# Token stage of a two-layer gated block: x2 turned as it is, routing logits from two sources, and new queue orders on all engines

## The chip, the cores and the metric

One core of a Trainium2 chip runs the kernel. The metric is device time in microseconds (us), the median of several runs. Names: TensorE (PE in the rows; PEld are its weight loads), VectorE (DVE), ScalarE (ACT), GpSimd (POOL), SyncE (SP, DMA queues). Semaphores order the engines; each engine works through its own queue in order.

## The reference, cut to what matters

All is fp32: x is (4, 2048, 512), ctx (4, 77, 512).

```python
x = x + tanh(g_xattn[0]) * memory_update(ctx, layernorm(x))   # a shift of rows, a strided convolution, ctx appended
x = x + tanh(g_ffn[0]) * quantised_linear(layernorm(x))       # blocks of 32 to a 6-bit grid, x @ w.T + bias   -> x2
Up = relu(layernorm(x) @ U_w.T); Uq = D_param * relu(ctx @ U_w.T)
x = x + tanh(g_xattn[1]) * softmax(mask(Up @ Uq.T)) @ ctx     # -> x3
t = layernorm(x)
idx, pmax = argmax, max of softmax(t @ Wr)                    # 8 experts
# each expert takes its first 1280 tokens; others keep t
x = x + tanh(g_ffn[1]) * pmax * (relu(t @ W1[idx]) @ W2[idx]) # or + tanh(..) * t for those without a place
```

## The kernel before

The kernel has a set-up, a token stage and an expert stage. The expert stage (`exp`, lines 1292 to 1790) is not touched. It starts when all engines have ended the block of the token stage.

**Token stage.** 8192 tokens go in 16 groups of 512, each as four tiles of 128 rows (T = 4). A software pipeline of six stages holds six groups at once: in step t, z is group t, a is t-1, b is t-2, c is t-3, d is t-4, e is t-5 (`groups`, line 198). Every engine has one `body(z, a, b, c, d, e)`, and `pipeline` (line 205) runs it: some steps written out, steps 6 to 15 as a loop, then the last five written out. Stage z normalises `xs`; a adds it to X, normalises into `n1` and quantises; b does the quantised linear and gives x2; c makes `up`; d scores, softmax and attention and gives x3; e writes t and x3 to memory and routes.

Products are split into fp32r high and low parts: ScalarE copies the high part out of PSUM, VectorE subtracts to get the low part, and TensorE multiplies three times (`split_terms`, line 713).

**TensorE's queue** in a step (`body`, line 721, order from about line 812): scores of d turned into p_sc (L727); `linear` x4 for b (12 products each, L710); `al` turned (L816); `attend` x4 for d; `turn_input` x4 for e (L718: four transposes each of the normalised `tt`); `project` x4 for c (12 products each, L780), with the fp32 `logits` of e (L763) inside `project(1)`; `turn_normed` x4 for b (the normalised `n2`, L718); positions of e (L838 to L842); scores of c (L710); `turn_quantised` x4 for a (L718).

**ScalarE's queue** (`body`, line 565): exponential of d, `alT_hi`, `tt` normalised, `n1` normalised, copies of the turned tiles (L574, L592), `up` (L583), `xs` normalised ahead of `up(1)` (L638), `n2` normalised, y, then the copies of the last turned tiles and `sT` (L669).

**VectorE's queue** (`body`, line 963): softmax sums, moments of d, a, c and b (`moments`, line 918: four `bn_stats` and four `bn_aggr`), the additions that make x2 (L974) and x3 (L987), quantisation (L1095 to L1108), low parts (L997, L1006), routing of e (L1074 to L1126), slots of the group before (`slots_of`, line 937).

**POOL** (line 473): X + xs (L480), slots scattered (L469), X + bias (L488), then dequantising `n1` (L494). **SP** loads `xs` and X when X + xs and x3 are done (`load_group`, line 361).

After the last step TensorE sums the counts (L914), and VectorE builds the tables of the expert stage (L1232 to L1281).

**Set-up** (lines 216 to 298 and the parts ahead of each `pipeline`): U_w and the linear weight are turned and split, keys `uq` and their low parts made, the convolution done.

## Time and profile before

| | us |
|---|---|
| median of 3 runs | 2196.72 (2196.54 to 2197.13) |
| the profiled execution | 2196.92 |
| its span, first to last instruction | 2194.6 |
| granted TensorE clock over the span | 0.961 of full speed |
| start to the first attention step | 172.3 |
| token stage up to the start of the experts | 874.7 |

The times in the rows are those of one profiled execution. "Idle before" is the time that an engine stood ahead of an instruction, with what released it. The duration of a matmul includes its way through the array, so what a matmul costs in a queue is the distance between starts. A clock of 1.00 is 2.4 GHz, 0.50 is 1.2 GHz.

### The profile page before, as it was taken

How to read it: one execution, taken by the hardware profiler on the slowest of the kernel's cores; microseconds unless marked ns; L12 is line 12 of the kernel's file. 1: busy time of each engine (PE TensorE's matmuls, PEld its weight loads, DVE VectorE, ACT ScalarE, POOL GpSimd, SP SyncE). 2: the span in 40 equal slices, each digit the busy share in tenths (PEclk: the TensorE clock that was granted, in tenths of full speed). 3: DMA queues.
4: the chain of work that ended last, by engine and by line, in shares of the span. 5: the costliest groups of instructions: out<-in, count | busy, mean ns of one | idle time of the engine just before them, and what ended most of it. 6: DMA issues, size and time to landing. Idle time of an engine off the chain costs nothing.

```text
span 2194.6 us, 35464 instructions
## 1 busy us (share of the span) xinstructions
PE 1982.1 (90%) x11356; PEld 1692.3 (77%) x11357; DVE 1043.4 (48%) x2321; ACT 794.8 (36%) x1548; POOL 670.9 (31%) x579
## 2 busy tenths in 40 slices
PE   4468998899889975799999999999999999999997
PEld 2456776677667754698988998899889899899986
DVE  3478888998899744424241115122413313322241
ACT  1254656555665443324141114111413313311241
POOL 0534243434353302415051115111513313301250
PEclk9689999999999985899999999999999999999999
DMA  6311333333333423615051004201512403301130
GB/s 190 112 61 43 122 130 121 116 120 140 115 120 121 146 85 117 197 32 185 20 183 43 29 29 156 69 29 38 183 43 91 129 29 96 120 19 38 54 112 16
DMA packets 152243, 208.41 MB, mean 95 GB/s; under 512 B 12831, under 2 KB 78623, under 8 KB 152198
## 3 DMA queue, kind: packets, MB, share of 16 engines
q1 hardware_dynamic: 111125, 114.14, 16.3%
q0 software_dynamic: 15728, 43.38, 6.5%
q10 hardware_dynamic: 25344, 50.33, 6.3%
q8 instruction: 22, 0.36, 0.1%
q14 instruction: 24, 0.19, 0.0%
HBM read 140.98 MB, written 68.37 MB: 95 GB/s over the span
## 4 chain that ended last, share of the span: by engine, by line
PE 58%; ACT 0%; issue 0%; DMA 0%; POOL 0%; POOLq 0%; DVEq 0%; ACTq 0%; DVE 0%
PE bank L1646 23%; PE bank L1654 22%; PE bank L1619 5%; PE bank L1599 5%; PE bank L1577 1%; PE bank L1608 1%; DMA tg<-t_d,idx_t 0%; ACT w_hi L1510 0%; PE bank L1583 0%; ACT w_hi L1511 0%; POOLq L1351 0%; DMA slots<-slot_d 0%; POOL out_dram L1389 0%; DVEq L1292 0%; ACT inT_hi L1496 0%
## 5 line engine op out<-in xcount | busy, mean ns | idle before, releaser
L1737 DVE SCALAR_TENSOR_TENSOR hT_lo<-bank,hT_hi 128x256 fp32r<-128x256 f32 x352 | 149.0, 423 | 657.0 <-ACT hT_hi L1541 657.0
L1541 ACT ACTIVATE hT_hi<-bank 128x256 fp32r<-128x256 f32 x352 | 135.1, 384 | 747.8 <-PE bank L1646 747.8
L1646 PE MATMUL bank<-inT_hi,w_lo 128*128 128x256 f32 x1408 | 398.5, 283 | 0.0
L1646 PE MATMUL bank<-inT_lo,w_hi 128*128 128x256 f32 x1408 | 398.3, 283 | 0.0
L1646 PE MATMUL bank<-inT_hi,w_hi 128*128 128x256 f32 x1408 | 396.8, 282 | 0.0
L1654 PE MATMUL bank<-w_hi,hT_hi 128*128 128x512 f32 x704 | 279.9, 398 | 0.0
L1646 PEld LDWEIGHTS bank<-inT_hi,w_hi 128*128 128x128 f32 x1408 | 269.0, 191 | 13.3
L1646 PEld LDWEIGHTS bank<-inT_lo,w_hi 128*128 128x128 f32 x1408 | 269.0, 191 | 12.0
L1654 PE MATMUL bank<-w_lo,hT_hi 128*128 128x512 f32 x704 | 277.7, 394 | 0.0
L1654 PE MATMUL bank<-w_hi,hT_lo 128*128 128x512 f32 x704 | 274.1, 389 | 0.0
L1646 PEld LDWEIGHTS bank<-inT_hi,w_lo 128*128 128x128 f32 x1408 | 269.0, 191 | 0.0
L1389 POOL DMA_INDIRECT out_dram<-ob,idx_x x46 | 46.5, 1010 | 633.9 <-DVE ob L1747 617.5
L1399 POOL TENSOR_TENSOR w_lo<-stage,w_hi 128x512 fp32r<-128x512 f32 x112 | 159.9, 1444 | 79.8 <-ACT w_hi L1510 79.7
L1654 PEld LDWEIGHTS bank<-w_hi,hT_lo 128*128 128x128 f32 x704 | 132.3, 188 | 30.1
L1654 PEld LDWEIGHTS bank<-w_hi,hT_hi 128*128 128x128 f32 x704 | 133.5, 190 | 17.4
L1654 PEld LDWEIGHTS bank<-w_lo,hT_hi 128*128 128x128 f32 x704 | 133.6, 190 | 15.2
L718 PE MATMUL bank<-ident,n 128*128 128x128 f32 x512 | 79.8, 290 | 72.0 <-POOL n L494 40.3
L469 POOL DMA_INDIRECT slot_d<-pay,flat x64 | 62.6, 979 | 266.2 <-DVE flat L959 251.6
L494 POOL TENSOR_TENSOR n<-q,s 128x512 f32<-128x512 fp8e4 x64 | 83.5, 1332 | 188.0 <-DVE q L1108 188.0
L1711 DVE TENSOR_TENSOR w_lo<-stage,w_hi 128x512 fp32r<-128x512 f32 x128 | 133.3, 1054 | 0.0
L718 PEld LDWEIGHTS bank<-ident,n 128*128 128x128 f32 x512 | 59.9, 148 | 93.8 <-issue 66.1
L780 PE MATMUL bank<-n2T_hi,uw_hi 128*128 128x512 f32 x256 | 110.2, 430 | 13.3 <-DVE up_lo L997 13.3
(266 smaller groups left out, 3931.5 us busy)
## 6 DMA issues: line engine op xcount, KB each, us to landing
stage<-in_L_ffn_W_dram SPq DMA_DIRECT2D x256, 256.0 KB, 3.6
...
```

What stands on the lines that cost most here:

```text
L469: pool.indirect_dma_start(out=slot_d, out_offset=bass.IndirectOffsetOnAxis(ap=flat[:, j:j + 1], axis=0), in_=pay[:, j, :], in_offset=None, ...
L494: pool.tensor_tensor(n1[:, j, :].rearrange("p (n c) -> p n c", c=BLK), q8[:, j, :].rearrange("p (n c) -> p n c", c=BLK), s64[:, j, :].unsq ...
L718: last = pe.transpose(dst_bank[:, k * P:k * P + P], src[:, j, k * P:k * P + P], ident[:, :])
L780: last = pe.matmul(u_banks[h % 2][:, :], l, rows_t, start=(k == 0 and n == 0), stop=(k == KB - 1 and n == 2))
L1399: pool.tensor_tensor(w1_lo[:, :, fs], w1_block(f), w1_hi[:, :, fs].bitcast(F32), ALU.subtract).then_inc(e_split[f % RING], 1)
L1541: act.activation(hT_hi[:, f % 4, :], hb[f % 4][:, 0:CN], ACT.Relu).then_inc(e_hh, 1)
L1599: last = pe.matmul(first_bank[q % 2][:, :], l[:, k, :], r[:, k, qs], start=(n == 0), stop=(n == 3 * KB - 1))
L1619: last = pe.matmul(unit_acc[:, :], l[:, q % 2, f, :], r[:, q * FQ + f, :], start=(q == 0 and n == 0), stop=(q == NF - 1 and n == 3 * FQ - 1))
L1646: last = pe.matmul(hb[f % 4][:, 0:CN], l[:, k, fs], r[:, k, :], start=(n == 0), stop=(n == 3 * KB - 1))
L1654: last = pe.matmul(acc[i][:, :], l[:, f % 4, js], r[:, f, :], start=(f == 0 and n == 0), stop=(f == FB - 1 and n == 2))
L1711: dve.tensor_tensor(w2_lo[:, f, :], w2_block(f), w2_hi[:, f, :].bitcast(F32), ALU.subtract).then_inc(e_split[f % RING], 1)
L1737: dve.scalar_tensor_tensor(out=hT_lo[:, f % 4, :], in0=hb[f % 4][:, 0:CN], scalar=0.0, in1=hT_hi[:, f % 4, :].bitcast(F32), op0=ALU.max, o ...
```

## The change

- **Normalised copies.** `n2` and the turned `tt` go. TensorE turns x2 itself (`turn_second`, from X). The mean is taken out of U_w and Wr in the set-up (their rows are centred), so products of x2 equal those of x2 less its mean. The factor 1/std of c is put into the scale of the softmax's exponential.
- **Statistics.** `bn_stats` of c and d go. The additions that make x2 and x3 also write their row sums (`accum_out`), and ScalarE sums squares of x minus mean (`squares`) and makes 1/std from them.
- **Logits.** They are the sum of two parts: turned x2 times centred Wr (`q_la`, 32 fp32r matmuls of 16 columns inside `project(1)`, for c) and the attention's weights times a table `cwr` = ctx @ Wr made in the set-up (`q_lb`, two matmuls in each `attend`). Argmax, one-hot, positions and counts are done with d, a step earlier than before; only 1/sum, slots and scatter stay with e.
- **Softmax.** Four exponentials read PSUM directly with a bias and a scale and give their sums.
- **Banks.** Attention has two PSUM banks, x2's turned tiles four.
- **Orders.** On all engines, below. VectorE now runs: scaled logits and y's factors of e, `add_linear(0)`, maximum of d, sum and slots of e, `add_linear(1)`, moments of a's X, `alT_lo` and softmax factors, `add_linear(2)`, `add_attention(0)`, `add_linear(3)`, `add_attention(1)`, quantisation with `up_rest(0)` in it, `add_attention(2)`, `up_rest(1)`, `add_attention(3)`, moments of `xs`, `up_rest(2)`, `a_m` and its like, routing of d, low parts of the quantised tiles with `up_rest(3)` after the second, those of x2, positions. POOL dequantises before it adds the bias, and scatters the slots of e in e's own step.
- **TensorE's steps** are all written out; it has no loop. The steps of the others are as before.
- **Set-up.** Two passes of ScalarE over `uf` ahead of its transposes; sums of keys and of Wr over partitions on TensorE; `uqf` from three VectorE operations instead of one; the table `cwr` (32 small matmuls) with its split.

```diff
+l_banks = q_banks = bank[1], bank[2]
+u_banks = bank[3], bank[0]
+o_banks = bank[5], bank[6]
+x_banks = bank[5], bank[6], bank[3], bank[0]
+b_s, b_sm = bank[4], bank[7]
+q_la = b_sm[:, 320:320 + T * 2 * E].rearrange("p (j w) -> p j w", j=T)
+q_lb = b_sm[:, 384:384 + T * 2 * E].rearrange("p (j w) -> p j w", j=T)
+p_pos = b_sm[:, 448:448 + T * E].rearrange("p (j e) -> p j e", j=T)
...
+def squares(x, g, nm, sq, s, told, spare):
+    wait(act, told, g + 1)
+    wait(act, s, T * g)
+    settled(act)
+    for j in range(T):
+        act.activation(spare[:, j, :], x(j).rearrange("p o d -> p (o d)"), ACT.Square, bias=nm[:, j:j + 1],
+                       accum_out=sq[:, j:j + 1]).then_inc(s, 1)
+def rstd_of_squares(kind, g, sq, s, rs):
+    wait(act, s, T * (g + 1))
+    act.activation(lv[kind][:, :], sq[:, :], ACT.Ln, bias=eps[:, :], scale=1.0 / D).then_inc(a_rs[kind], 1)
+    wait(act, a_rs[kind], 2 * g + 1)
+    settled(act)
+    act.activation(rs, lv[kind][:, :], ACT.Exp, scale=-0.5).then_inc(a_rs[kind], 1)
...
+    wait(act, v_re, 3 * e + 1)
+    act.activation(re_[:, :, :], rsc[:, :, :], ACT.Exp).then_inc(a_re, 1)
+    wait(act, v_ys, 3 * e + 1)
+    wait(act, s_t, 16 * e)
+    settled(act)
+    for j in range(T):
+        act.activation(tt[:, j, :], x3[:, ds(xe + j, 1), :], ACT.Identity, bias=nb_d[:, j:j + 1],
+                       scale=rs_d[:, j:j + 1]).then_inc(a_tt, 1)
 if d is not None:
+    wait(act, v_sm, 3 * d + 2)
+    settled(act)
+    for j in range(T):
+        act.activation(al[:, j, :], p_sc[:, j, :], ACT.Exp, bias=nbx[:, j:j + 1],
+                       scale=rs_c[:, ds((d % T) * T + j, 1)], accum_out=ssm[:, j:j + 1]).then_inc(a_al, 1)
+if e is not None:
+    wait(act, a_tt, T * (e + 1))
+    act.dma_start(t_d[ds(er, G), :].rearrange("(j p) e -> p j e", p=P), tt[:, :, :]).then_inc(s_t, 16)
 if d is not None:
     wait(act, p_ca, d + 1)
     wait(act, p_co, T * d)
+    wait(act, p_lb, d)
     act.activation(alT_hi[:, :], b_s[0:L, :], ACT.Copy).then_inc(a_th, 1)
 if a is not None:
     rstd("b", a)
     wait(act, v_ln["b"], LN * (a + 1))
     wait(act, p_bt, T * a)
     normed("b", n1, lambda j: X[:, ds((a % T) * T + j, 1), :], a_n1)
 if e is not None:
     if d is not None:
         wait(act, v_x3, T * d + 1)
     act.dma_start(x3_d[ds(er, G), :].rearrange("(j p) e -> p j e", p=P),
                   x3[:, ds(xe, T), :]).then_inc(s_x3, 16)
+    wait(act, v_ys, 3 * (e + 1))
     wait(act, s_y, 16 * e)
     settled(act)
     for j in range(T):
         act.activation(y[:, j, :], x3[:, ds(xe + j, 1), :], ACT.Identity, bias=y_nb[:, j:j + 1],
                        scale=y_sc[:, j:j + 1]).then_inc(a_y, 1)
+up(0)
+if e is not None:
     wait(act, a_y, T * (e + 1))
     act.dma_start(of[ds(er, G), :].rearrange("(j p) e -> p j e", p=P), y[:, :, :]).then_inc(s_y, 16)
+if b is not None:
+    squares(lambda j: X[:, ds((b % T) * T + j, 1), :], b, nm_c, sq_c, a_sq, v_nm, junk)
+up(1)
+if b is not None:
+    rstd_of_squares("c", b, sq_c, a_sq, rs_c[:, ds((b % T) * T, T)])
+up(2)
+if d is not None:
+    squares(lambda j: x3[:, ds((d % 2) * T + j, 1), :], d, nm_d, sq_d, a_sd, v_nd, junk_d)
+if z is not None:
+    rstd("a", z)
+up(3)
+if d is not None:
+    rstd_of_squares("d", d, sq_d, a_sd, rs_d[:, :])
+if z is not None:
+    wait(act, v_ln["a"], (LN + 2) * (z + 1))
+    for j in range(T):
+        act.activation(xs[:, j, :], xs[:, j, :], ACT.Identity, bias=ln["a"][3][:, j:j + 1],
+                       scale=a_sc[:, j:j + 1]).then_inc(a_u, 1)
+for j in range(T):
+    quantised_hi(j)
+for j in range(T):
+    second_hi(j)
 if c is not None:
     wait(act, p_cs, c + 1)
     wait(act, p_cr, c)
     act.activation(sT[:, :], b_s[0:L, :], ACT.Identity, bias=maskb[:, ds(c, 1)]).then_inc(a_st, 1)
...
+    wait(pe, v_bl, T * b + (j + 3 if j < 2 else j + 1))
...
+        if d > 0:
+            wait(pe, v_r, 8 * (d - 1) + 1)
+    if j >= 2:
+        wait(pe, v_x3, T * d + j - 1)
+    elif c is not None:
+        wait(pe, v_cl, T * c + j + 1)
+    product(o_banks[j % 2][:, :], split_terms(alT_hi[:, js], alT_lo[:, js], cxb[:, 0, :], cxb[:, 1, :])
+    pe.matmul(q_lb[:, j, :], alT_hi[:, js], cwr[:, d // NQ, :], start=True, stop=False, skip_group_check=True)
+    last = pe.matmul(q_lb[:, j, :], alT_lo[:, js], cwr[:, d // NQ, :], start=False, stop=True,
+                     skip_group_check=True)
+    if j == T - 1:
+        last.then_inc(p_lb, 1)
...
+    js = slice(j * P, j * P + P)
+    for k in range(KB):
+        for part in (x2T_hi, x2T_lo):
+            last = pe.matmul(q_la[:, j, :], part[:, k, js], wr_hl[:, k, :], start=(k == 0 and part is x2T_hi),
+                             stop=(k == KB - 1 and part is x2T_lo), skip_group_check=True)
+    if j == T - 1:
+        last.then_inc(p_la, 1)
...
+def turn_second(j):
+    if b is None:
+        return
+    wait(pe, v_x2, T * (b + 1))
+    if d is not None and j < 2:
+        wait(pe, v_x3, T * d + 3 + j)
+    if c is not None and j >= 2:
+        wait(pe, v_ul, KB * c + 1 + j)
+    for k in range(KB):
+        last = pe.transpose(x_banks[j][:, k * P:k * P + P], X[:, (b % T) * T + j, k * P:k * P + P],
+                            ident[:, :])
+    last.then_inc(p_ct, 1)
...
 linear(0)
 if d is not None:
+    wait(pe, a_st, d + 1)
+    if d >= 1:
+        wait(pe, v_pp, 7 * (d - 1) + 1)
     for j in range(T):
+        last = pe.transpose(p_sc[:, j, :], sT[:, j * P:j * P + P], ident[0:L, 0:L])
+    last.then_inc(p_cr, 1)
+linear(1)
+if d is not None:
+    for j in range(T):
+        wait(pe, a_al, T * d + j + 1)
         last = pe.transpose(b_s[0:L, j * P:j * P + P], al[:, j, :], ident[:, :])
     last.then_inc(p_ca, 1)
+linear(2)
 attend(0)
+linear(3)
 attend(1)
+project(0)
 attend(2)
+project(1, logits)
 attend(3)
 project(2)
+turn_quantised(0)
+turn_quantised(1)
 project(3)
+turn_quantised(2)
+turn_quantised(3)
+for j in range(T):
+    turn_second(j)
+if d is not None:
+    wait(pe, v_oh, 3 * d + 2)
+    if c is not None:
+        wait(pe, v_la, c + 1)
...
+    slots_of(e)
+add_linear(1)
+if a is not None:
+    wait(dve, g_x1, a + 1)
+    moments("b", a, lambda j: tile_of(a, j))
 if d is not None:
     wait(dve, a_th, d + 1)
     dve.tensor_tensor(alT_lo[:, :], b_s[0:L, :], alT_hi[:, :].bitcast(F32), ALU.subtract).then_inc(v_tl, 1)
+    wait(dve, a_al, T * (d + 1))
     dve.reciprocal(srd[:, :], ssm[:, :]).then_inc(v_sm, 1)
+    wait(dve, v_sm, 3 * d + 3)
     dve.tensor_scalar(scf[:, :], srd[:, :], gx[:, ds(d, 1)], None, ALU.mult).then_inc(v_scf, 1)
+add_linear(2)
...
+act.wait_ge(l_uf, 16)
+for k in range(KB):
+    act.activation(uf[:, k, :], uf[:, k, :], ACT.Copy, accum_out=us[:, k:k + 1]).then_inc(k_act, 1)
+act.wait_ge(k_act, act_at[f"us{KB - 1}"])
+act.activation(unm[:, :], us[:, :], ACT.Copy, scale=-1.0 / D).then_inc(k_act, 1)
+act.activation(umean[:, :], us[:, :], ACT.Copy, scale=1.0 / D).then_inc(k_act, 1)
+act.wait_ge(k_act, act_at["unm"])
+for k in range(KB):
+    act.activation(uf[:, k, :], uf[:, k, :], ACT.Identity, bias=unm[:, k:k + 1]).then_inc(k_act, 1)
...
+pe.wait_ge(k_dve, dve_at["wrlo"])
+for b in range(B):
+    for k in range(KB):
+        for part in (cxT_hi, cxT_lo):
+            last = pe.matmul(cwr_bank[:, b, :], part[:, k, b * L:b * L + L], wr_hl[:, k, :],
+                             start=(k == 0 and part is cxT_hi), stop=(k == KB - 1 and part is cxT_lo),
+                             skip_group_check=True)
+last.then_inc(k_pe, 1)
```

## Rows read from the trace of the kernel before

**Rows 1.** the page: busy us (share of the span) of each engine

```profile
PE 1982.1 (90%) x11356; PEld 1692.3 (77%) x11357; DVE 1043.4 (48%) x2321; ACT 794.8 (36%) x1548; POOL 670.9 (31%) x579
```

**Rows 2.** busy time in steps: window, us, engines (instructions), TensorE clock, DMA

```profile
172.29:213.04 40.75, 35.33 (x161) 27.06 (x161) 31.22 (x66) 18.33 (x34) 14.82 (x7) 0.96 0.15 52
213.04:256.28 43.24, 39.46 (x213) 31.34 (x214) 36.28 (x90) 27.07 (x49) 15.28 (x7) 1.00 0.34 123
256.28:302.16 45.88, 41.19 (x215) 32.40 (x214) 39.56 (x100) 27.12 (x49) 18.55 (x11) 0.96 0.37 122
346.41:390.66 44.25, 39.68 (x215) 31.34 (x214) 39.37 (x100) 26.97 (x49) 18.24 (x11) 1.00 0.34 119
700.37:743.51 43.14, 39.27 (x215) 31.34 (x214) 34.42 (x89) 23.74 (x43) 16.03 (x10) 1.00 0.28 98
743.51:783.06 39.55, 36.73 (x200) 29.68 (x198) 23.40 (x68) 18.73 (x34) 3.91 (x4) 1.00 0.46 145
783.06:817.56 34.50, 28.09 (x133) 21.28 (x133) 14.20 (x49) 12.66 (x22) 3.87 (x4) 0.85 0.24 86
817.56:874.70 57.14, 29.72 (x128) 24.92 (x128) 26.51 (x118) 18.55 (x32) 12.16 (x16) 0.53 0.35 125
```

**Rows 3.** waits of TensorE in nine full steps: us, times, longest

```profile
PE bank L710 <- DVE up_lo L997: 12.4, 9, 1.4
...
PE bank L718 <- DVE n2T_lo L1006: 4.6, 9, 0.5
```

**Rows 4.** timeline of TensorE in one step: start, us, instructions

```profile
411.46 0.96 PE L763 MATMUL bank<-wr_sb,tT 128*128 128x8 f32 x8
412.27 0.48 PE L780 MATMUL bank<-n2T_hi,uw_hi 128*128 128x512 f32 x1
...
423.66 1.03 PE L718 MATMUL bank<-ident,n 128*128 128x128 f32 x8
424.54 0.18 PE L838 MATMUL bank<-ohb,tri 128*128 128x32 bf16 x1
...
435.55 0.49 PE L710 MATMUL bank<-wd_hi,xdT_hi 128*128 128x512 f32 x1
...
438.40 0.60 PE L816 MATMUL bank<-ident,al 128*77 128x128 f32 x4
```

**Rows 5.** timeline of ScalarE in the same step

```profile
413.12 0.30 ACT L555 ACTIVATE lv_a<-mv_a,eps 128x4 f32<-128x4 f32 x1 [1.57 <-DVE mv_a L928]
413.45 0.21 ACT L557 ACTIVATE rs_a<-lv_a 128x4 f32<-128x4 f32 x1
416.12 2.93 ACT L638 ACTIVATE xs<-xs,nb_a,a_sc 128x512 f32<-128x512 f32 x4 [2.46 <-DVE nb_a L1062]
...
424.48 1.07 ACT L574 ACTIVATE n2T_hi<-bank 128x512 fp32r<-128x512 f32 x2
```

**Rows 6.** groups of VectorE, 400 to 584 us: busy us, mean ns

```profile
L924 DVE BATCH_NORM_STATS2 st_d<-x 128x6 f32 x16 | 9.8, 678 | 0.0
...
L1059 DVE TENSOR_TENSOR a_m<-rs_a,mg 128x4 f32<-128x4 f32 x4 | 7.4, 1845 | 3.1 <-ACT rs_a L557 3.1
```

**Rows 7.** two waits of TensorE, and a stretch with its clock

```profile
158.81 0.79 PE L780 MATMUL bank<-n2T_hi,uw_hi 128*128 128x512 f32 x1 [4.13 <-DVE up_lo L997]
...
199.02 0.67 PE L780 MATMUL bank<-n2T_hi,uw_hi 128*128 128x512 f32 x1 [3.43 <-DVE up_lo L997]
...
158.10:161.50 3.40, 2.69 (x6) 2.15 (x7) 3.40 (x7) 3.06 (x5) 0.00 (x0) 0.52 0.00 0
```

**Rows 8.** timeline of VectorE at the stage's end

```profile
863.54 0.17 DVE L1232 MEMSET n<- 128x128 f32 x1
...
872.52 0.14 DVE L1281 CAST tables<-n 1x1 int32<-1x1 f32 x1
```

**Rows 9.** timeline of VectorE in the set-up

```profile
86.06 2.47 DVE L924 BATCH_NORM_STATS2 st_a<-xs 128x6 f32<-128x512 f32 x4 [9.43 <-DMA xs<-comp_d]
```

**Rows 10.** timeline of ScalarE in the set-up

```profile
0.88 1.28 ACT L673 ACT_TABLE_LOAD   x1 [0.72 <-PEq L1800]
```

More of the change, by code:

```diff
@@ L203, in groups, with pipeline @@
             return tuple(t - n if 0 <= t - n < NG else None for n in range(STAGES))
-        def pipeline(eng, body, first):
+        def pipeline(eng, body, first, end=STEPS):
             for t in range(first, STAGES):
@@ L211, in pipeline @@
                 body(*groups(t))
-            for t in range(NG, STEPS):
+            for t in range(NG, end):
                 body(*groups(t))
@@ L721, in body @@
             def body(z, a, b, c, d, e):
-                if d is not None:
-                    wait(pe, a_st, d + 1)
-                    if not isinstance(d, int) or d >= 2:
-                        wait(pe, v_pp, 7 * (d - 2) + 1)
-                    for j in range(T):
-                        last = pe.transpose(p_sc[:, j, :], sT[:, j * P:j * P + P], ident[0:L, 0:L])
-                    last.then_inc(p_cr, 1)
                 def linear(j):
@@ L753, in attend @@
                             ).then_inc(p_co, 1)
-                def logits(j):
-                    if e is None:
-                        return
-                    wait(pe, a_tT, T * e + j + 1)
-                    if j == 0 and d is not None:
-                        wait(pe, v_sm, 4 * d + 2)
-                    for k in range(KB):
-                        last = pe.matmul(p_lg[:, j, :], tT[:, k, j * P:j * P + P], wr_sb[:, k, :],
-                                         start=(k == 0), stop=(k == KB - 1), skip_group_check=True)
-                    if j == T - 1:
-                        last.then_inc(p_dl, 1)
@@ L889, in _ @@
                 transposes(f"cxT{k}", [(slice(b * L, b * L + L), cx[:, b, k * P:k * P + P]) for b in range(B)])
+            pe.wait_ge(k_dve, dve_at["cxT3"])
+            for k in range(KB):
+                for c in (cxT_hi, cxT_lo):
+                    last = pe.matmul(bank[bank_of["keysum"]][:, 0:B * L], onesr[:, :], c[:, k, :],
+                                     start=(k == 0 and c is cxT_hi), stop=(k == KB - 1 and c is cxT_lo))
+            last.then_inc(k_pe, 1)
+            pe.wait_ge(l_wr, 16)
+            for k in range(KB):
+                last = pe.matmul(wr_total, onesf[:, :], wr_sb[:, k, :], start=(k == 0), stop=(k == KB - 1),
+                                 skip_group_check=True)
+            last.then_inc(k_pe, 1)
             for h in range(KB):
@@ L971, in add_linear @@
                         wait(dve, g_xb, b + 1)
+                        wait(dve, v_nm, b)
                     wait(dve, p_bm, T * b + j + 1)
@@ L1042, in body @@
                 add_attention(1)
                 if a is not None:
-                    shift("b", a)
-                if e is not None and (not isinstance(e, int) or e >= 1):
-                    slots_of(e - 1)
-                add_linear(3)
-                add_attention(2)
-                up_rest(0)
+                    for j in range(T):
+                        wait(dve, a_n1, T * a + j + 1)
+                        dve.tensor_reduce(ab[:, j, :], n1[:, j, :].rearrange("p (n c) -> p n c", c=BLK), AX.X, ALU.max,
+                                          apply_absolute_value=True).then_inc(v_ab, 1)
@@ L1134, in _ @@
+                if d is not None:
+                    wait(dve, p_dp, d + 1)
+                    dve.tensor_tensor(rpe[:, :, :], p_pos[:, :, :], oh[:, :, :], ALU.mult).then_inc(v_pp, 1)
+                    wait(dve, v_pp, 7 * d + 1)
+                    dve.tensor_reduce(pos[:, :], rpe[:, :, :], AX.X, ALU.add).then_inc(v_pp, 1)
             done = [0]
```

457 lines of the change are left out of this document (209 added, 248 removed).

## The prediction

> **What bounds the kernel now.** I read the page's busy shares first [rows 1]: TensorE holds 90% of the span. The change touches only the token stage, from the start to 874.7 us, so everything below is read there. A table by step [rows 2], cut at the transposes that open each step, shows the rhythm: a full step takes 44.25 us with TensorE busy 39.7 and VectorE 39.4 of it, at full clock; the first two full-size steps take 40.75 and 43.24, the next 45.88; the last ones 43.14, 39.55, 34.50, and 57.14 us pass from the last attention step to the start of the experts. The waits of TensorE over nine full steps (five rows of the view of waits, of which [rows 3] are the first and the last) add up to 38 us, 4.3 a step: 2.0 for the low parts of `up`, 1.6 for those of the turned copies, 0.7 for POOL. So a step is TensorE's queue plus short waits for a VectorE that is nearly full, and a change must shorten TensorE's queue without lengthening a wait.
>
> **Prices.** Starts of neighbouring rows [rows 4] give what an instruction holds TensorE for: 12 products of 128x512 take 2.85 us (435.55 to 438.40), eight transposes 0.88 (423.66 to 424.54), eight weight-load and matmul pairs of the fp32 logits 0.81 (411.46 to 412.27). ScalarE [rows 5]: four 128x512 pieces from SBUF 2.93, two from PSUM 1.07 (0.54 each), a statistic 0.30 and then 0.21. VectorE [rows 6]: `bn_stats` of 128x512 0.68 (four and their aggregates 2.7), `a_m` 1.85 on 128x4.
>
> **TensorE's queue.** Removed: four `turn_input` a step, 4 x 0.44 = 1.8, and about 0.4 of changes between transposes and products. The fp32 logits ran as 32 pairs, 4 x 0.81 = 3.2. The new ones are 32 fp32r matmuls of 16 columns, which the trace does not have: from below the old pairs' 0.10 less the little that their 8 columns take, from above a full product's 0.24 (which would add 4.5 us a step); I keep 0.10, 3.2 in all, because like the old ones they are a full weight load with almost no columns. Added: eight such pairs in `attend`, 0.8. So the queue of a full step is linear and project 8 x 2.85 = 22.8, attention 2.8, scores 2.8, eight turned tiles 3.5, `sT` and `al` 0.8, small matmuls 4.1: 36.8 us against 39.7. That is 2.9 us less a step, if nothing waits.
>
> **What waits instead.** I place the new orders against each other from the start of `linear(0)`. VectorE now does the moments of the next group (2.7) before `alT_lo`; it ends near 10.2, and `attend(0)`, which could start at 9.1, waits 1.1. `project(2)` ends at about 28.6. Behind it ScalarE's queue is: `up(2)` 0.5, four squares of x3 2.9, the statistic of a 0.5, `up(3)` 0.5, the statistic of d 0.5, `xs` normalised 2.9, and only then `quantised_hi(0)` 0.6; VectorE's low part takes another 0.7. TensorE's `turn_quantised(2)` waits for exactly that low part (its bank is read until then), since both first tiles have been turned before `project(3)`. With gaps the chain ends at 38.2; `project(3)` ends at 32.3. So TensorE stands 5.9 us in one piece, and everything behind it in the queue (two quantised tiles, four of x2, the positions, the scores, the next `linear`) waits with it. After the wait come 0.44 + 0.3 + 0.44, 4 x 0.44 and 2.8, 5.8 us, and the step ends at 44.0. In the old order `xs` stood ahead of `up(1)`, where it hid behind `project`; that is the cover that is gone.
>
> The squares, the exponentials and two kinds of sums now write an accumulator. No row shows what that costs; the nearest are the small operations, from 0 (folded in) to 0.30 each on ScalarE [rows 5]. I take 0.15: four squares lie on the chain, +0.6; on VectorE two sums lie before `alT_lo`, below 0.2. With that a step is 44.5 us (43.8 to 45.5), against 44.25: TensorE's saving is given back whole. The Trainium skill, page "VectorE: DVE Perf Modes", section "Two Vector instructions with no wait between them", says that an operation that also writes its accumulator out is two instructions, the second an accumulator read; no run here shows it yet. By it the sums of VectorE are not free either; with a folded-in read the step would be 43.8.
>
> VectorE itself loses the moments of c and d (5.4), the subtraction and the sum of the softmax (0.9), and probably `a_m`'s wait beside POOL (1.7), and gains about 1.6 of small ones: near 33 us of 44, no bound. ScalarE goes from 27 to about 31.
>
> **The clock.** The rows show what a wait of this size does here [rows 7]: TensorE stood 4.13 us before 158.81 and 3.43 before 199.02, the granted clock was 0.52 in the stretch from 158.10 to 161.50 (1.2 instead of 2.4 GHz), and products then took 0.63 to 0.79. The waits of up to 1.4 us in full steps left it at 1.00 [rows 2]. A wait of 6 us in every step should therefore end at the low level each time. The work behind it then runs at half speed for the 3.4 us of those rows or somewhat longer: 1.7 us lost at least, 3.4 if the low level lasts twice as long. I take 1.9, for part of it is hidden where transposes wait for ScalarE anyway. A full step is then 46.4 us.
>
> A rule that speaks against the change stands in the Trainium skill, page "TensorE: Matmul & The Clock Gate", section "HAM oscillation — how this bites in real kernels": a wait repeated in every tile throttles the array every time, so the ramp is paid per tile and not once. The rows agree for single waits; the steps before the change never had one that long. By the rule the sum is the 46.4; without it the 44.5.
>
> **The edges.** Set-up gains TensorE work (8 key sums, 8 passes of router sums and 32 pairs for the context-router table; at 0.1 to 0.24 each 5 to 11 us), two passes of ScalarE over `uf`, and VectorE operations. The passes hide behind the convolution and VectorE's work on `wf`. The table delays `uqlo` and VectorE's first body by about 11 us; but that body used to wait for `xs` until 86.06 [rows 9] with the quantisation behind it, and now quantises first, so most is hidden. With a shorter second step (POOL now dequantises before the bias) and the new wait in the third, the first attention step starts 3 us later (-4 to +8).
>
> The steps without `xs` (the last three) lose the long wait: about 41.2, 36.5 and 32, 7.4 us less than the 117.2 of [rows 2]. The last step turned four tiles, did the logits, positions and counts on TensorE, and the last table was begun at 872.52 [rows 8]. Now the counts are final one step earlier. From the last `sT` (817.56), as estimates from the prices above: 4.8 to `attend(0)`, 4 x 1.7 at the low clock, then sum, squares and statistic 4.8, the scaled logits, exponential, slots 3.3, and 9.1 for the tables (863.54 to the end of the last row): 28.8 instead of 55.1, so 26 less. The DMA of `y` leaves near 23.6 and lands in time.
>
> **The sum.** All against the profiled execution, 2196.92 us with a span of 2194.6; the median of the runs is 2196.72, 0.2 lower. Start +3.0; step with d alone 46.4 - 40.75 = +5.6; next 46.4 - 43.24 = +3.2; next 46.4 - 45.88 = +0.5; nine full steps 9 x 2.15 = +19.4; last three -7.4; end -26. Together -1.7: 2195.2, and by the median **2195.0 us**.
>
> **Rivals.** (1) The long wait is there, but the clock holds, or the low stretch falls mostly on hidden transposes: 12 x 1.9 = 23 less, **2172**. Against it speak both rows of [rows 7]. (2) The wait is not there, because ScalarE gets through its queue earlier than I place it: then the step is TensorE's 36.8 and the 1.1 and some gaps, 39 to 40, some 5 us less than now in ten steps: with the edges about **2120**. For it speaks that ScalarE is busy 27 of 44 us; against it that the queue is in order and cannot start before `project(2)` ends. (3) The other side: the chain behind `project(2)` is longer or the clock stays low through the scores. Each 0.1 us of an accumulator read costs 0.4 a step and twice the low stretch 1.5. At a step of 48.0 the total is 2195 + 12 x 1.6 = **2214**; from 46.9 on the kernel is slower by over 0.2%. (4) The change does not do what it says: were `Square` not in the loaded table set, each step would pay table loads, of 1.28 us each [rows 10], well over 2230. Nothing in the trace shows a reload among the functions used.
>
> **Chances.** Forecast (2185 to 2207) 0.42; (1) 0.20; (2) 0.10; (3) 0.25; (4) 0.03. The range from 2155 to 2214 holds the forecast, (1) with its short accumulator (10 less) and (3) up to its price, and leaves out (2) and (4). About 0.2% (4.4 us) is what a measurement of this kernel can tell from no change. The forecast's own range gives 0.15 faster, 0.15 same, 0.12 slower; (1) and (2) are faster; (3) is slower but for a small part. Together 0.45 faster, 0.18 same, 0.37 slower. Both signs are open: the likeliest case alone is 2185 to 2207.
>
> **What would show it.** In the profile after: a wait of 5 to 7 us of TensorE before the third quantised tile of each full step, released by `xdT_lo`; the granted clock near 0.5 right after it and a mean of 0.9 over these steps; full steps of 46 us; `attend(0)` waiting about 1 us for `alT_lo`; accumulator reads as rows of their own or not; tables some 26 us sooner after the last `sT`. The prediction is wrong if that wait is under 2 us, or if the clock is 1.00 in spite of it.

## The result, and the profile after

| | before | after |
|---|---|---|
| median | 2196.63 us | 2233.72 us (2229.25 to 2235.53) |
| the profiled execution, its span | 2196.92, 2194.6 | 2233.29, 2231.6 |
| granted TensorE clock over the span | 0.961 | 0.943 |

After takes 1.0166 times as long (95% interval 1.0148 to 1.0183): 1.7% or 37 us slower, outside the range of 2155 to 2214. The page's busy time and share of the span:

```profile
PE 1981.0 (89%) x11276; PEld 1712.4 (77%) x11277; DVE 1011.4 (45%) x2286; ACT 830.3 (37%) x1805; POOL 671.5 (30%) x579
```

The table by step, cut at the transposes of `sT` (columns as in [rows 2]): the first attention step, a full one, and the three without `xs`.

```profile
195.28:242.13 46.85, 39.89 (x206) 33.11 (x205) 34.67 (x84) 24.86 (x58) 14.35 (x6) 0.93 0.13 42
...
529.06:576.90 47.84, 39.98 (x207) 32.91 (x206) 36.51 (x96) 28.94 (x64) 18.26 (x10) 0.93 0.39 139
768.07:809.62 41.55, 37.49 (x206) 30.65 (x205) 32.37 (x85) 25.32 (x58) 13.71 (x9) 1.00 0.28 102
809.62:843.90 34.28, 32.73 (x178) 26.71 (x176) 17.19 (x62) 17.77 (x46) 3.93 (x4) 1.00 0.46 154
843.90:879.59 35.69, 29.02 (x125) 22.05 (x125) 11.70 (x49) 14.21 (x35) 3.89 (x4) 0.81 0.24 89
```

A full step went from 44.25 us [rows 2] to 47.8, and its clock from 1.00 to 0.93. With `xs` gone (768.07) a step falls to 41.55 at clock 1.00. TensorE's timeline shows where the time of a full step lies: the last product of `project(3)`, then a wait.

```profile
559.04 0.40 PE L820 MATMUL bank<-x2T_hi,uw_lo 128*128 128x512 f32 x1
566.30 1.94 PE L759 MATMUL bank<-ident,n 128*128 128x128 f32 x8 [6.86 <-DVE xdT_lo L1071]
568.03 3.32 PE L836 MATMUL bank<-ident,X 128*128 128x128 f32 x16
```

Three stretches behind it (columns as above) show the granted clock: 0.5, that is 1.2 GHz, until the transposes are done, and 2.4 GHz for the scores.

```profile
564.00:568.00 4.00, 1.70 (x8) 1.73 (x9) 2.09 (x5) 2.49 (x5) 2.72 (x1) 0.51 0.00 0
568.00:571.00 3.00, 3.00 (x17) 3.00 (x16) 2.46 (x4) 1.98 (x5) 1.82 (x1) 0.52 0.02 5
571.00:574.00 3.00, 3.00 (x21) 2.04 (x19) 2.38 (x9) 0.98 (x2) 0.00 (x0) 1.00 0.90 298
```

ScalarE's queue in the same step, from the timeline. TensorE waits for `xdT_lo` of VectorE, which needs `xdT_hi` of ScalarE, and everything between `up_hi` at 555.81 and `xdT_hi` at 564.85 stands ahead of that copy.

```profile
555.81 0.60 ACT L599 ACTIVATE up_hi<-bank 128x512 fp32r<-128x512 f32 x1 [3.42 <-PE bank L820]
557.78 0.72 ACT L582 ACTIVATE junk_d<-x,nm_d 128x512 f32 x1 [1.36 <-DVE nm_d L1146]
558.40 0.19 ACT L582 ACTIVATION_READ_ACCUMULATOR junk_d<-x,nm_d 128x1 f32 x1
558.50 0.71 ACT L582 ACTIVATE junk_d<-x,nm_d 128x512 f32 x1
...
560.62 0.28 ACT L566 ACTIVATE lv_a<-mv_a,eps 128x4 f32<-128x4 f32 x1
560.93 0.20 ACT L568 ACTIVATE rs_a<-lv_a 128x4 f32<-128x4 f32 x1
561.04 0.58 ACT L599 ACTIVATE up_hi<-bank 128x512 fp32r<-128x512 f32 x1
...
562.03 2.91 ACT L686 ACTIVATE xs<-xs,nb_a,a_sc 128x512 f32<-128x512 f32 x4
564.85 1.05 ACT L607 ACTIVATE xdT_hi<-bank 128x512 fp32r<-128x512 f32 x2
```

The squares started 1.36 us late, for `nm_d`. That is a 128x4 operation of VectorE. Its row and POOL's beside it, from their timelines:

```profile
552.85 4.62 POOL L507 TENSOR_TENSOR X<-X,gbias 128x2048 f32 x1
...
553.82 3.68 DVE L1146 TENSOR_SCALAR nm_d<-sum_d 128x4 f32<-128x4 f32 x1
```

`nm_d` ends at 557.50, POOL's addition at 557.47. The same thing stands in the set-up and the first bodies (timeline of VectorE and POOL):

```profile
66.07 5.40 DVE L1276 TENSOR_SCALAR X<-X,dp 128x308 f32<-128x308 f32 x1
66.78 4.51 POOL L491 TENSOR_TENSOR X<-X,xs 128x2048 f32<-128x2048 f32 x1
...
87.96 0.22 DVE L1299 TENSOR_REDUCE cwf<-bank 77x32 f32<-77x64 f32 x1 [4.42 <-PE bank L961]
...
90.15 2.46 DVE L984 BATCH_NORM_STATS2 st_b<-X 128x6 f32<-128x512 f32 x4
...
104.50 4.49 POOL L507 TENSOR_TENSOR X<-X,gbias 128x2048 f32<-128x2048 f32 x1
...
105.94 3.07 DVE L1157 TENSOR_TENSOR a_m<-rs_a,mg 128x4 f32<-128x4 f32 x1 [0.60 <-ACT rs_a L568]
...
112.41 4.53 POOL L491 TENSOR_TENSOR X<-X,xs 128x2048 f32<-128x2048 f32 x1 [3.42 <-issue]
```

And TensorE stands the same long wait, before the third quantised tile, in each of the first three bodies too (its timeline); none of the first three bodies of before has a wait for `xdT_lo` over 0.5 us:

```profile
113.59 1.94 PE L759 MATMUL bank<-ident,n 128*128 128x128 f32 x8 [10.34 <-DVE xdT_lo L1071]
...
148.78 1.94 PE L759 MATMUL bank<-ident,n 128*128 128x128 f32 x8 [10.34 <-DVE xdT_lo L1071]
...
185.64 1.94 PE L759 MATMUL bank<-ident,n 128*128 128x128 f32 x8 [4.80 <-DVE xdT_lo L1071]
```

VectorE's first body starts at 90.15 instead of 73.00 us, the second addition of `xs` at 112.41 instead of 99.30, and the first `sT` comes at 195.28 instead of 172.29 [rows 2] (2.85 of that is only `linear(0)`, which now stands ahead of it). The end went as forecast: from the last `sT` (879.59) to the end of the last table (908.73) 29.1 us pass, against 55.1.

### The profile page after: what moved, and what is told of

Its sections match the earlier page's. It is cut to its first block, busy times and chain, and to the rows that moved or that the text cites. A ratio compares the mean times of both kernels' runs of the same rounds, so it can differ in the third digit from the quotient of the medians.

```text
span 2231.6 us, 35225 instructions
## 1 busy us (share of the span) xinstructions
PE 1981.0 (89%) x11276; PEld 1712.4 (77%) x11277; DVE 1011.4 (45%) x2286; ACT 830.3 (37%) x1805; POOL 671.5 (30%) x579
## 4 chain that ended last, share of the span: by engine, by line
PE 57%; ACT 0%; issue 0%; DMA 0%; POOL 0%; POOLq 0%; DVEq 0%; ACTq 0%; DVE 0%
PE bank L1737 23%; PE bank L1745 22%; PE bank L1710 5%; PE bank L1690 5%; PE bank L1668 1%; PE bank L1699 1%; DMA tg<-t_d,idx_t 0%; PE bank L1674 0%; ACT w_hi L1601 0%; ACT w_hi L1602 0%; POOLq L1442 0%; DMA slots<-slot_d 0%; POOL out_dram L1480 0%; DVEq L1383 0%; ACT inT_hi L1587 0%
## 5 line engine op out<-in xcount | busy, mean ns | idle before, releaser
L759 PE MATMUL bank<-ident,n 128*128 128x128 f32 x256 | 49.3, 354 | 129.9 <-DVE xdT_lo L1071 109.9
L759 PEld LDWEIGHTS bank<-ident,n 128*128 128x128 f32 x256 | 40.3, 184 | 139.7 <-issue 116.5
L820 PE MATMUL bank<-x2T_hi,uw_hi 128*128 128x512 f32 x256 | 110.7, 432 | 0.0
```

The source lines that it names most:

```text
L759: last = pe.transpose(dst_bank[:, k * P:k * P + P], src[:, j, k * P:k * P + P], ident[:, :])
L820: last = pe.matmul(u_banks[h % 2][:, :], l, rows_t, start=(k == 0 and n == 0), stop=(k == KB - 1 and n == 2))
```

## The experiments

All numbers are device us. "Full step" is the mean of the nine full steps, from one `sT` to the next. The ratio is to the kernel before on the same chip.

| | median | ratio, 95% interval | first sT | full step |
|---|---|---|---|---|
| before | 2196.63 | | 172.29 | 44.25 |
| after | 2233.72 | 1.0166 (1.0148 to 1.0183) | 195.28 | 47.83 |
| e1 high parts early | 2157.50 | 0.9819 (0.9798 to 0.9839) | 181.37 | 42.84 |
| e2 nm_d in another form | 2231.55 | 1.0147 (1.0130 to 1.0164) | 196.28 | 47.84 |
| e3 xs late | 2218.93 | 1.0093 (1.0076 to 1.0110) | 184.42 | 47.73 |
| e4 wait filled | 2209.91 | 1.0049 (1.0032 to 1.0066) | 196.57 | 45.76 |
| e5 POOL in pieces | 2213.43 | 1.0072 (1.0055 to 1.0089) | 191.96 | 46.30 |
| e6 table later | 2228.33 | 1.0135 (1.0118 to 1.0152) | 190.42 | 47.84 |
| e7 orders mended | 2133.06 | 0.9702 (0.9686 to 0.9718) | 180.14 | 40.96 |
| e8 and alT_lo, table | 2127.80 | 0.9675 (0.9659 to 0.9692) | 174.81 | 41.04 |
| e9 and tt behind | 2099.59 | 0.9554 (0.9539 to 0.9569) | 171.56 | 39.13 |
| e10 e8, order back | 2187.96 | 0.9953 (0.9937 to 0.9968) | 187.56 | 44.41 |
| e11 before, pieces | 2204.07 | 1.0028 (1.0017 to 1.0040) | 171.33 | 44.77 |
| e12 e9, POOL whole | 2148.01 | 0.9764 (0.9745 to 0.9783) | 182.34 | 42.19 |
| e13 nm_d on ScalarE | 2224.49 | 1.0119 (1.0102 to 1.0135) | 193.40 | 47.12 |
| e14 e12, nm_d on ScalarE | 2099.58 | 0.9547 (0.9531 to 0.9563) | 181.91 | 38.55 |
| e15 e9, nm_d on ScalarE | 2097.96 | 0.9547 (0.9531 to 0.9563) | 173.81 | 39.03 |

**e1: the order alone.** ScalarE; on VectorE the first two `turned_rest` went behind `up_rest(2)`.

```diff
 up(2)
+quantised_hi(0)
+quantised_hi(1)
 squares(x3 ...); rstd("a", z); up(3); rstd_of_squares("d", d, ...); xs normalised
-for j in range(T):
-    quantised_hi(j)
+quantised_hi(2)
+quantised_hi(3)
```

> The changed kernel with one thing moved: ScalarE copies the high parts of the first two quantised tiles right behind up(2), ahead of the squares of x3, and VectorE makes their low parts right behind up_rest(2). In the changed kernel (median 2233.7) TensorE stands 6.86 us before the third quantised tile in every full step of 47.8 us, and the granted clock then is 0.5 for 6.8 us. Theory A (the order of ScalarE's queue): the wait goes, the clock stays at 1.00 in full steps, and what is late next is the one-hot matrix of the routing (VectorE had it at 564.2, TensorE would be ready near 562.3). Steps of 40.5 to 42 us, so 12 steps times 6 to 7 us: 2150 to 2162. Theory B (ScalarE and VectorE have too much to do in any order): the wait only moves, to the next linear(0), which needs three low parts; steps of 46 us or more, 2210 to 2233.

76 us came back, more than the whole loss. In the profiled executions 13.9 of them lie ahead of the first `sT` (181.37 instead of 195.28), 45 in the nine full steps. The long wait split into two short ones, and the clock stayed at 1.00 (a full step, columns as above; then TensorE's waits longer than 1 us in it):

```profile
523.60:566.44 42.84, 38.09 (x206) 30.62 (x205) 36.02 (x96) 28.54 (x64) 18.33 (x10) 1.00 0.36 123
```

```profile
556.13 1.23 PE L761 MATMUL bank<-ident,n 128*128 128x128 f32 x8 [2.13 <-DVE xdT_lo L1073]
...
560.26 0.63 PE L838 MATMUL bank<-ident,X 128*128 128x128 f32 x4 [1.60 <-DVE up_lo L1064]
```

The step is 0.8 us over the top of theory A's span: the quantised tile's low part still stood behind `nm_d` and the moments, and `up(3)` behind the squares. Theory B falls.

**e4: the clock's own price.** Ahead of `turn_quantised(2)`; nobody reads the products.

```diff
+if a is not None and d is not None:
+    wait(pe, v_x3, T * (d + 1))
+    for _ in range(24):
+        pe.matmul(o_banks[0][:, :], uw_hi[:, 0, 0:P], wd_hi[:, 0, :], start=True, stop=True)
 turn_quantised(2)
```

> The changed kernel with 24 matmuls of 128x512 more on TensorE (24 x 0.235 = 5.6 us at full clock), between project(3) and the third quantised tile, where it stands 6.86 us; nobody reads their result. They lie inside the wait, so it ends at the same moment. Theory A (the low clock behind the wait costs 1.9 us a step on its own): the clock stays at 1.00 in full steps, the stretch from the end of the wait to the scores' end goes from 7.75 to about 5.8 us, 12 x 1.9 = 23 less: 2207 to 2214. Theory B (the transposes behind the wait are paced by ScalarE and VectorE anyway): the clock stays up and the time does not move, 2230 to 2236.

```profile
544.70 5.65 PE L879 MATMUL bank<-wd_hi,uw_hi 128*128 128x512 f32 x24
551.74 1.23 PE L759 MATMUL bank<-ident,n 128*128 128x128 f32 x8 [1.39 <-DVE xdT_lo L1075]
552.80 1.91 PE L836 MATMUL bank<-ident,X 128*128 128x128 f32 x16
```

Work added, 24 us less: the third quantised tile came as late after `sT` as before (37.2 us), the 16 transposes took 1.91 instead of 3.32, and a full step lost 2.07 us at clock 1.00. So of the 47.8 us of a step 2.1 are the low clock; the prediction had 1.9. Theory A stands.

**e3: one piece of the chain moved.** `xs` normalised behind `second_hi(3)`.

> The changed kernel with the normalisation of xs on ScalarE (four pieces, 2.9 us) moved from ahead of quantised_hi(0) to behind the copies of the turned x2. Theory A (each piece of the chain ahead of quantised_hi(0) costs its duration): the wait of TensorE goes from 6.9 to 4.0 us; the clock still falls for one stretch of a few us, as it did for single waits of 3.4 and 4.1 us; steps of 44.9, 12 x 2.9 = 35 less: 2195 to 2203. Theory A with the clock held by the shorter wait: 2 us a step more, 2175 to 2180. Theory B (POOL then adds xs to X so late that the moments of that group on VectorE, and attend(0) behind them, wait): less than half the gain, 2215 or more.

Theory A fell. Theory B's number came (2215 or more), but not by its way: `attend(0)` waited 0.9 us as before. The full step moved by 0.1 us; the 15 us came in the first steps (first `sT` 10.9 sooner), where `xs` had stood between `a_m` and `xdT_hi` (109.32 and 112.15 in after). In a full step the copy was made early, and VectorE was late (ScalarE, VectorE, TensorE):

```profile
596.23 1.08 ACT L607 ACTIVATE xdT_hi<-bank 128x512 fp32r<-128x512 f32 x2
...
595.98 0.22 DVE L1166 TENSOR_REDUCE lb<-bank 128x32 f32<-128x64 f32 x1
...
598.44 1.28 DVE L1071 TENSOR_TENSOR xdT_lo<-bank,xdT_hi 128x512 fp32r<-128x512 f32 x2
...
599.27 1.94 PE L759 MATMUL bank<-ident,n 128*128 128x128 f32 x8 [5.64 <-DVE xdT_lo L1071]
```

The routing of d (from 595.98) stands ahead of `xdT_lo` on VectorE. So there is a second chain, 1.2 us shorter than ScalarE's. The wait fell by those 1.2 us, and they were lost again: 0.3 in the 16 transposes at the low clock (3.62 us instead of 3.32), 0.4 in a new wait for `al`, which `xs` now stands ahead of; the rest is not resolved. So in a full step moving `xs` alone gains almost nothing. e1 moved the low parts on both engines.

**e2: nm_d in another form.**

```diff
-dve.tensor_scalar(nm_d, sum_d, -1.0 / D, None, ALU.mult)
+dve.scalar_tensor_tensor(out=nm_d, in0=sum_d, scalar=-1.0 / D, in1=ones[:, 0:T], op0=ALU.mult, op1=ALU.mult)
```

> The changed kernel with the negative mean of x3, nm_d (128x4), written as a scalar_tensor_tensor (times a row of ones) instead of a tensor_scalar. It took 3.68 us in every full step and ended with POOL's bias addition (553.82 + 3.68 = 557.50; 552.85 + 4.62 = 557.47), and the squares of x3 waited 1.36 us for it. Theory A (it is this form of instruction that waits for POOL): 0.16 us, the chain behind it is 1.3 us shorter, 12 steps: 2216 to 2220. Theory B (any small operation there waits for POOL, or the next one does in its place): nm_d still 3 us or more, or bn_stats behind it grows by as much; 2230 to 2236.

```profile
L1146 DVE SCALAR_TENSOR_TENSOR nm_d<-sum_d,ones 128x4 f32<-128x4 f32 x4 | 14.7, 3677 | 0.1
L984 DVE BATCH_NORM_STATS2 st_b<-X 128x6 f32 x16 | 9.9, 680 | 0.0
L984 DVE BATCH_NORM_STATS2 st_a<-xs 128x6 f32<-128x512 f32 x16 | 9.8, 672 | 0.0
```

3677 ns a time (groups of VectorE: busy, mean ns), theory B: the form made no difference. But not every instruction of VectorE waits: in e13 four `bn_stats` took their usual 2.47 us (from 545.94) wholly under POOL's addition (544.89 to 549.51). The Trainium skill, page "SBUF — State Buffer", section "Who interferes with whom", says that VectorE and GpSimd share a port pair, which a VectorE instruction needs in a two-port mode (`tensor_scalar` can enter one) or with two SBUF inputs, and that whoever issues first has it for its whole instruction. Both forms of e2 are of these kinds: by that page the edit was bound to fail, and the rows agree.

**e5: POOL's two additions in four instructions each.**

> The changed kernel with POOL's two large additions (X + xs and X + bias, 128x2048, 4.6 us each) written as four instructions of 128x512 each. In the changed kernel nm_d (128x4 on VectorE) ended with the bias addition, 3.68 us after its start, a_m in the first body likewise (3.07 us), and uqf (128x308) in the set-up with X + xs (5.40 us). Theory A (some VectorE instructions wait for the POOL instruction that is running, and for no more): none of them takes over 1.4 us; the first sT transpose comes 5 to 8 us sooner (195.3 before), the full step loses the 1.36 us that the squares waited for nm_d: 12 x 1.3 = 16; in all 2209 to 2216. Theory B (they wait until POOL is idle, or share with it all along): nm_d still 3 us or more, 2230 or above.

20 us less, a step 1.5 us shorter, `nm_d` 0.35 us instead of 3.68. Theory A, but not its limit of 1.4 us: `uqf` still took 3.38 us, from 66.54, over two pieces. First `sT` 3.3 sooner, not 5 to 8.

**e6: the table's last steps behind the first body.**

> The changed kernel with the last two steps of the context-router table (cwf and cwlo on VectorE, cwhi on ScalarE) moved behind the first body, and uqlo ahead of them. VectorE's first body began at 90.15 us, behind a wait of 4.42 us for the table's matmuls. Theory A (set-up ahead of the first body is paid in full, since the quantisation now stands ahead of the moments of xs and nothing else covers it): the body starts 4.5 to 5 us sooner, and so does the first sT transpose (195.28): 2228 to 2230. Theory B (the wait for xs covers it, as the prediction had it): first sT within 1 us, 2233.

VectorE's first body started at 84.57 instead of 90.15, and the first `sT` came 4.9 us sooner: nothing covered it.

**e7 and e8: the orders mended.** On top of e1 and e5, ScalarE runs squares of x3, `quantised_hi(0)`, `quantised_hi(1)`, `up(2)`; VectorE makes `up_rest(3)` ahead of the routing; TensorE does the scores ahead of the positions. e8 adds `alT_lo` ahead of the moments, and e6's edit.

> The changed kernel with the ScalarE order of the first experiment carried further, and POOL's additions in four pieces: ScalarE runs the squares of x3, quantised_hi(0), quantised_hi(1), up(2), statistic of a, up(3), statistic of d, xs; VectorE makes the two low parts ahead of up_rest(2), and up_rest(3) ahead of the routing; TensorE does the scores ahead of the positions. The first experiment (2157.5, full steps of 42.8 us) still had TensorE waiting 2.1 us for xdT_lo and 1.6 us for up_lo(3) in a step, beside 0.9 for alT_lo. Theory A (what is left are these orders and the nm_d that POOL holds): both waits under 0.5 us, steps of 39 to 40 us, 2110 to 2125. Theory B (VectorE with 36 and ScalarE with 29 us of work are too full for steps under 42): waits of the same size at other places, 2145 to 2157.

> The kernel of the seventh experiment, with alT_lo ahead of the moments of the next group on VectorE, and with the table's last steps behind the first body. Theory A: attend(0) no longer waits (0.9 us in each of 15 steps), and the first steps come some 4.5 us sooner: 15 to 18 us less than the seventh. Theory B (the 0.9 comes back as a later n1 and quantisation, and the table is hidden): within 5 us of the seventh.

The waits for `xdT_lo` and `up_lo` are gone, but in e7 a full step is 41.0, 1 us over theory A, and the median 8 us over it, for a new wait: ScalarE normalises `tt` ahead of the exponentials. e8 is 5.3 us faster than e7, near theory B's figure and far from A's 15 to 18. These 5.3 are just its earlier first `sT` (5.3), so the table is not hidden, as B had it; `alT_lo` gave nothing in a full step. Timeline of TensorE in e8, then stretches with the clock:

```profile
504.01 1.68 PE L868 MATMUL bank<-ident,al 128*77 128x128 f32 x4 [1.51 <-ACT al L641]
```

```profile
504.00:506.00 2.00, 1.80 (x6) 1.14 (x7) 1.10 (x6) 1.42 (x7) 0.93 (x1) 0.78 1.06 344
506.00:508.00 2.00, 2.00 (x6) 1.57 (x5) 1.64 (x3) 0.32 (x1) 1.39 (x3) 0.50 0.95 364
508.00:510.00 2.00, 2.00 (x9) 1.59 (x8) 1.85 (x8) 0.21 (x1) 1.58 (x2) 0.87 0.02 1
```

**e9: tt behind alT_hi.**

> The kernel of the eighth experiment with ScalarE's four pieces of tt (2.93 us) moved from ahead of the exponentials al to behind alT_hi. The eighth (2127.8, full steps of 41.0 us) has TensorE waiting 1.51 us for al in a full step, and a mean granted clock of 0.91 in the 20 us around it (1.00 in the next 20). Theory A (the wait alone is the last thing between it and its queue, and brings the clock down): no wait for al, clock 1.00, steps of 38 to 39 us, 14 steps times 2 to 3 us: 2087 to 2100. Theory B (tt then delays the statistic and n1, and the quantisation with them; POOL's and VectorE's chain is the next bound): 2115 or more.

28 us less. A full step of e9, with TensorE busy 37.9 of 39.1 us:

```profile
481.64:520.78 39.14, 37.94 (x205) 30.53 (x206) 33.71 (x97) 28.04 (x63) 19.20 (x17) 1.00 0.38 134
```

**e10: the one order put back into e8.**

> The kernel of the eighth experiment with one order put back: ScalarE copies the high parts of the first two quantised tiles behind up(3), the statistic of d and xs again, and VectorE makes their low parts behind the routing. Theory A (this order alone makes the long wait, whatever else is mended): TensorE stands 5 to 6 us before the third quantised tile, the clock is at 0.5 behind it, steps of 47 to 49 us, 12 times 6 to 8 us: 2200 to 2224, as slow as the changed kernel less what the set-up and nm_d give. Theory B (the wait of the changed kernel came as much from nm_d and POOL): wait under 4 us, below 2190.

```profile
489.69 1.94 PE L763 MATMUL bank<-ident,n 128*128 128x128 f32 x8 [5.32 <-DVE xdT_lo L1075]
```

60 us lost by this order alone, 12.8 of them ahead of the first `sT`. The wait is the 5.3 us of theory A, while the median lies where theory B put it: the step is shorter than A said (44.4, not 47 to 49), since e8's wait for `al`, and the low clock behind that, went when TensorE came later.

**e11: the pieces in the kernel before.**

> The kernel before with POOL's two additions in four pieces each, nothing else. There a_m (128x4) took 1.85 us on VectorE in a full step, and TensorE waited 4.3 us a step, mostly for VectorE. Theory A (an instruction of VectorE waits for the running POOL instruction in this kernel too): a_m under 1 us, and as it lies on no wait of TensorE, the time moves by less than 0.2%: 2192 to 2199. Theory B (the 1.2 us saved reach TensorE): 11 steps times 1.2, 2183 to 2187. Theory C (four pieces take longer than one, and X comes later): up to 0.4 us a step, 2198 to 2203.

0.28% slower, nearest to theory C. `a_m` took longer than its 1.84 us, to the end of all four pieces (VectorE, POOL):

```profile
503.86 2.24 DVE L1063 TENSOR_TENSOR a_m<-rs_a,mg 128x4 f32<-128x4 f32 x1 [0.77 <-ACT rs_a L561]
...
501.08 4.99 POOL L491 TENSOR_TENSOR X<-X,gbias 128x512 f32 x4
```

The four pieces take 0.4 us more than the one, and a full step grew by 0.5; that the one makes the other is likely and not shown. That an instruction of VectorE gets through at the next border of two pieces is not certain then: `nm_d` did, `a_m` here and `uqf` in e5 did not. What decides it stays open.

**e12: POOL whole again in e9.**

> The kernel of the ninth experiment (2099.6, full steps of 39.1 us) with POOL's two additions as one instruction of 128x2048 each again. Theory A (nm_d waits for the whole addition again, over 3 us, and here the squares and, behind them, quantised_hi(0) wait with it): TensorE waits 2 to 3 us for xdT_lo, and the clock may fall with it; full steps of 41.5 to 44 us, 2130 to 2160. Theory B (here as in the kernel before the wait costs nothing on TensorE, and one instruction instead of four is 0.4 us shorter): 2090 to 2100.

```profile
500.71 4.18 DVE L1150 TENSOR_SCALAR nm_d<-sum_d 128x4 f32<-128x4 f32 x1
...
509.45 1.23 PE L762 MATMUL bank<-ident,n 128*128 128x128 f32 x8 [3.12 <-DVE xdT_lo L1074]
```

48 us: 10.8 up to the first `sT`, and 3.1 in a full step, since the squares and `quantised_hi(0)` stand behind `nm_d` here.

**e13 to e15: nm_d on ScalarE.**

```diff
-dve.tensor_scalar(nm_d, sum_d, -1.0 / D, None, ALU.mult)
+act.activation(nm_d, sum_d, ACT.Copy, scale=-1.0 / D)     # ahead of squares(x3)
```

> The changed kernel with nm_d computed on ScalarE (128x4, a copy with scale -1/512, right ahead of the squares) instead of VectorE; POOL's additions whole. Theory A (the port that POOL holds is VectorE's alone, ScalarE does not wait): nm_d 0.2 us, the squares of x3 start 1.1 us sooner (they stood 1.36 us), VectorE's moments of xs 3.5 us sooner; steps of 46.5 to 46.8 us against 47.8: 12 to 16 us less, 2217 to 2222. Theory B (nm_d is no part of the chain; the queue of ScalarE behind it sets the wait anyway): steps of 47.8, 2230 to 2236.

> The kernel of the twelfth experiment (all orders mended, POOL's additions whole, 2148.0) with nm_d computed on ScalarE. Theory A (all of the 48 us between the ninth, with pieces, and the twelfth is nm_d's wait for the bias addition): they come back without the pieces, steps of 38.9 to 39.2 us, 2088 to 2101. Theory B (other VectorE instructions wait for POOL's whole additions here too, such as a_m): steps of 40 us or more, 2112 or above.

> The kernel of the ninth experiment (all orders mended, POOL's additions in pieces, 2099.6) with nm_d computed on ScalarE, where it takes 0.87 us on VectorE. TensorE is busy 37.9 of 39.1 us there and waits only 0.8 us for al and 0.2 for VectorE. Theory A (TensorE's own queue is the bound, the chain behind nm_d is hidden): 2094 to 2102, the ninth again. Theory B (the chain behind nm_d still reaches TensorE): over 6 us less.

In e13 it takes 0.2 us, the squares start at once, and a full step loses 0.7 us, about half of what was expected (single ones from 45.9 to 47.7); the time lies between the two theories. With POOL's additions whole and `nm_d` on ScalarE (e14) all 48 us come back, as theory A had it, but not all where e12 lost them: the first `sT` is only 0.4 us sooner than in e12, and a full step is 3.6 us shorter, 0.6 shorter than in e9. That the sum meets e9's median is in part luck. So in full steps the pieces helped through `nm_d` alone, and whole additions are 0.3 us a step better (38.55 against 38.9 in eight of the nine steps of e15; its ninth took 40.42, which nothing here explains); up to the first `sT`, where `uqf` and `a_m` wait, the pieces are worth 8 us (173.81 against 181.91). e15 is e9 again: the chain is hidden, TensorE's queue is the bound. e9, e14 and e15, at 0.955 of the kernel before, are the fastest.

## Why the prediction was wrong

It said 2195.0 and was 39 us too low. By its own terms, from step start to step start in the two profiled executions (in after a step starts 2.85 us ahead of its `sT` as long as there is a `linear(0)`):

| term | predicted | measured |
|---|---|---|
| start to the first attention step | +3.0 | +20.1 |
| step with d alone, next, next | +5.6, +3.2, +0.5 | +6.1, +4.0, +2.3 |
| nine full steps | +19.4 (9 x 2.15) | +32.3 (9 x 3.59) |
| three steps without xs | -7.4 | -2.8 |
| the end | -26 | -26.0 |
| sum | -1.7 | +36.0 |

**The mechanism was right.** The long wait of a full step is where it was put, released by `xdT_lo`; the clock falls behind it; `attend(0)` waits 0.9 us for `alT_lo` (1.1 predicted). The rivals without the wait or with the clock held (1 and 2) are out. What came is rival 3: the step of 47.8 us is within its price of 48.0, and what took the time past its 2214 are the start (17.1 us more than predicted) and the last three steps (4.6 more). That the kernel would be slower had a chance of 0.37.

**The start is the step that failed: +3.0 us was predicted, +20.1 came.** Two things were said of it. "Most is hidden" was so in part: VectorE's first body starts 17.2 us later (11 predicted), and TensorE turns its first quantised tile at 100.69 us instead of 95.58, only 5.1 later. But the quantisation that now stands ahead of the moments already fills the time in which the old body waited for `xs` [rows 9], so nothing is left to hide more: e6 starts the body 5.6 us sooner and has its first `sT` 4.9 sooner. The other was "the new wait in the third" step. It stands in all three, 10.34, 10.34 and 4.80 us. The chain that was added up for a full step holds in the first bodies as well: there `xdT_hi` stands behind the moments of `xs`, `a_m` (3.07 us, for POOL's addition) and `xs`, and was not priced. The experiments show it both ways: e1, the order alone, gives 13.9 of the 20.1 us back, and what is left, 6.2, is inside the -4 to +8 that was stated; e10, the same order put back, costs 12.8. The single pieces are 10.9 for `xs` out of the queue (e3), 4.9 for the table (e6) and 3.3 for POOL's port (e5); they overlap with e1, and all of them with the other orders (e8) give 20.5.

**The full step: 47.8, not 46.4.** Of the 1.4 us, 0.9 are TensorE's queue up to the end of `project(3)` (33.2 us from `linear(0)`, not 32.3) and 0.5 the wait (6.9, where 5.9 and 0.5 for the accumulators stood); the 7.7 us behind it are what was said. The queue was summed too short: 39.7 less the 2.2 that were removed and plus the 0.8 that were added is 38.3, not 36.8. Measured are 38.0: 47.83 less the waits (6.86 and 0.87) and the 2.07 of e4; and e14, which waits little more than 0.5 us a step, needs 38.55. In the wait the term at fault is POOL: VectorE was to lose "probably `a_m`'s wait beside POOL (1.7)". It did, for `a_m` is 0.16 us now. The wait went to `nm_d`, which the new order of POOL puts under the bias addition, at the head of the very chain that was added up. It holds the squares for 1.36 us; with it on ScalarE (e13) they start 1.0 us sooner behind `up_hi`. The port rule cited at e2 was not weighed, and `nm_d` beside POOL had no term at all.

**The last steps and the end.** The last three steps lost 2.8 us, not 7.4. The first of them still has a wait of 3.10 us for `xdT_lo`. But most of the miss is the very last, 35.7 us where 32 was said. No `linear(0)` stands there between `sT` and the turning of `al`, and TensorE waited 2.85 us (1.57 before) for the exponentials behind `tt`; with `tt` behind them that step went from 34.65 (e8) to 32.73 us (e9). The 26.0 us of the end are right to the tenth partly by luck: `attend(0)` came 6.4 us after the last `sT`, not 4.8, and from the end of the attention to the tables it took 6.8 us, not 8.1.

**The accumulator** was priced at 0.15 an operation, 0.6 on the chain. Reads are rows of their own on both engines, on VectorE of 0.08 us:

```profile
530.13 0.08 DVE L1038 DVE_READ_ACCUMULATOR X<-bank,gates,X 128x1 f32 x1
```

The page "VectorE: DVE Perf Modes" of the Trainium skill, section "Two Vector instructions with no wait between them", has it so for VectorE. On ScalarE they fit beside the next square: from start to next start four squares take 2.84 us (557.78 to 560.62), and four plain pieces 2.82 (562.03 to 564.85). On the chain the price is nothing. That hid nearly half of what `nm_d` cost.

**The clock** was priced at 1.9 us a step from two waits of the set-up [rows 7]; e4 measures 2.07. The rule of the Trainium skill that was weighed there (page "TensorE: Matmul & The Clock Gate", section "HAM oscillation — how this bites in real kernels") holds for the wait of 6.86 us, which pays in every full step. It does not hold for every repeated wait: e1 has 2.13 us in each step at a clock of 1.00.
